# What TensorE waits for in two attention loops: a later exponential in place of a one-element fence

## The chip, the cores and the metric

One Trainium2 chip, all 8 cores, the same program on each with its own batch element of 4096 tokens. The metric is the device time in microseconds of the slowest core, as the median over runs. The span is the time from the first to the last instruction of the profiled execution on the slowest core.

## The reference

For each of 8 batch elements x is 4096 x 1024. First comes full attention with 16 heads of 64, then a two-layer block with windowed attention and a gated feed-forward:

```python
def _L0_attn_ref(query, Wq, Wk, Wv, Wp, bp):
    q = einsum('bnd,hde->bhne', query, Wq) * (1 / sqrt(E))
    k = einsum('bmd,hde->bhme', query, Wk); v = einsum('bmd,hde->bhme', query, Wv)
    attn = softmax(einsum('bhne,bhme->bhnm', q, k), axis=-1)
    out = einsum('bhnm,bhme->bnhe', attn, v)
    return dot(swapaxes(out, -1, -2).reshape(B, N, E * H), Wp) + bp
def _layer(x, ...):                      # DEPTH = 2, 8 heads of 64, window 512
    h = shift_token(x); q, k, v = split(h @ wqkv, 3)
    q, k = rotary_xpos(l2norm(q) * qs, l2norm(k) * ksc)
    x = x + local_attention(q, k, v) @ wo          # own window and the one before it
    a, g = split(layernorm(shift_token(x)) @ w1 + b1, 2)
    return x + (a * gelu(g)) @ w2 + b2
x = x + _L0_attn_ref(_layernorm(x), ...)
x = x + _L0_ffn_ref(_layernorm(x), ...)            # two times _layer
```

## The kernel before, in words

The program is written engine by engine. Each call of `op` (line 131) appends one instruction to the list of one engine, in the order of the code, and an engine works its list in order. Engines meet on counting semaphores: T for TensorE (`'T'`), V for VectorE (`'V'`), S for ScalarE (`'S'`). A `wait` list names a semaphore and the value that it has to reach. `self.val('S')` is the value that S will have after everything put on ScalarE's list so far. On VectorE and ScalarE `op` adds two things to each instruction: it waits until the one before it on the same engine is complete, and it raises the engine's own semaphore by one when it is complete. All instructions have line 150 in the profile, since `op` issues them, so they are told apart by their tiles.

A fence (`sfence` on ScalarE, `vfence` on VectorE) copies one element of the tile `fsc` onto another. A consumer that waits for the value after the fence waits for the instruction ahead of it and for the copy.

Stage A (`_stage_a`, from line 364 on) normalises x into eight tiles h, then goes over 4 groups of 4 heads. Per group it loads the weights, computes K (tiles KTg) and V (tile Vg) for all 4096 tokens, and goes over 8 blocks of 512 queries. Per block it projects Q for two pairs of heads (tile Qg) and runs one attention loop per pair. After both loops come eight output projections (Ost with Wpg), each followed by work of VectorE and a DMA.

An attention loop has 32 chunks of 128 keys, with mc as the counter. Per chunk:

- Q·K: two matmuls (KTg with Qg, 64 rows each, one for each head) into pb1 for even chunks and pb3 for odd ones. They wait for the value `sexp[mc - 2]`, since that exponential read the same buffer.
- Exponential: one ACTIVATE of 128 x 1024 from the buffer into Pa (even) or Pb (odd), which waits for the Q·K pair and for the P·V pair of chunk mc - 2, which read the same tile.
- P·V: two matmuls (Vg with Pa or Pb) that accumulate in pb5 and pb6 over all chunks. They wait for `sexp[j]`.

The code of iteration mc puts Q·K of chunk mc on TensorE's list, then P·V of chunk mc - 1. The list so reads QK0, QK1, PV0, QK2, PV1, QK3, PV2 and so on. `sexp[mc]` is set to the value after a fence (line 601). When the loop is over, VectorE takes the reciprocal of the row of sums (RECIPROCAL into drow), TensorE spreads it over 64 partitions, and VectorE scales the result; so for both heads.

Stage F (`_ffn_layer`, from line 741 on, called once for each of two layers) goes over 8 windows of 512 tokens, with projections, norms and rotation, and then 4 pairs of heads of local attention. Per pair there are 8 chunks of 128 keys, 4 in window 0. Per chunk k: two Q·K matmuls (kf with qf) into pb5 and pb6 for even k, into pb1 for odd k, which wait for `sexp_l[k - 2]`; two additions of a 128 x 128 mask by VectorE in place and a VectorE fence; two ACTIVATEs (into the Ph tiles, 128 to 512 columns each) that wait for this fence; a ScalarE fence, whose value is `sexp_l[k]` (line 1100). After the last chunk TensorE waits for `self.val('S')` (line 1103) and does all P·V matmuls of the pair. Then come reciprocal, spreading and scaling as in stage A. The rest of a layer is the output projection, statistics, and a feed-forward over 16 spans of 256 tokens.

Of the kernel before, what the change touches and what calls it, by code (L numbers as in the profile page):

```python
# [8 lines left out]
F32 = mybir.dt.float32  # L9
# [88 lines left out]
class MK:  # L98
# [106 lines left out]
    def build(self):  # L205
        nc = self.nc
        with self.es:
            self._declare_dram()
            self._globals()
            blk = self.es.enter_context(nc.Block())  # L210
            self._stage_a()
            if self.stage in ('F0', 'F0q'):
                self._ffn_layer(0)
            elif self.stage not in ('A', 'A0'):
                self._ffn_layer(0)
                self._ffn_layer(1)
            self._finish()
            with nc.allow_low_precision(reason="bf16 matmul operands by design"):
                for tag, attr in [('T', 'tensor'), ('V', 'vector'), ('S', 'scalar'),
                                  ('G', 'gpsimd'), ('Y', 'sync')]:  # L220
                    fns = self.q[tag]
                    def body(eng, fns=fns):
                        for fn in fns:
                            fn(eng)
                    getattr(blk, attr)(body)
        return nc
# [137 lines left out]
    def _stage_a(self):  # L364
# [10 lines left out]
        pOa, pOb, pm = self.pb5, self.pb6, self.pb7  # L375
# [5 lines left out]
        stA = self.stA = contextlib.ExitStack()  # L381
# [10 lines left out]
        for s in range(8):  # L392
# [11 lines left out]
            for c in range(NCH):  # L404
                for ms in range(4):
                    st = (s == 0 and c == 0 and ms == 0)
# [8 lines left out]
                            inc=(('T', 1) if last else None))  # L415
# [15 lines left out]
        for s in range(8):  # L431
# [14 lines left out]
            for c in range(NCH):  # L446
# [4 lines left out]
                        inc=(('V', 1) if c == NCH - 1 else None))  # L451
# [14 lines left out]
        Vg4 = Vg.rearrange("p (m h e) -> p m h e", h=4, e=65)  # L466
# [5 lines left out]
        Pa = self.sbuf('Pa', [128, 1024], BF16, st=stA)  # L472
        Pb = self.sbuf('Pb', [128, 1024], BF16, st=stA)
        dn = self.sbuf('dn', [64, 512], F32, st=stA)
        drow = self.sbuf('drow', [1, 512], BF16, st=stA)
        Ost = self.sbuf('Ost', [128, 2 * 512], BF16, st=stA)
        ysb = [self.sbuf(f'ysb{i}', [128, 512], F32, st=stA) for i in range(2)]
        yac = [self.sbuf(f'yac{i}', [128, 512], F32, st=stA) for i in range(2)]
# [12 lines left out]
        for grp in range(ngrp):  # L491
# [71 lines left out]
            for qb in range(NQB):  # L563
                if qb == 1:
                    self.canary(2 + grp * 3)
                for p in range(2):
                    for c in range(NCH):
                        self.op('T', 'matmul', pm[:, :], Wq_g[c][:, p * 128:(p + 1) * 128],
                                h[c][:, qb * 512:(qb + 1) * 512],
                                start=(c == 0), stop=(c == NCH - 1),  # L570
                                inc=(('T', 1) if c == NCH - 1 else None))
# [4 lines left out]
                for p in range(2):  # L576
                    sexp = {}
                    tavm = {}
                    p0exp = self.val('S')
                    for mc in range(33):  # L580
                        if mc < 32:
                            Sp = pb1 if mc % 2 == 0 else pb3
                            Pj = Pa if mc % 2 == 0 else Pb
                            wS = [('S', sexp[mc - 2])] if mc >= 2 else [('S', p0exp)]
                            self.op('T', 'matmul', Sp[:, 0:512],
                                    KT[p][0:64, mc * 128:(mc + 1) * 128],
                                    Qg[0:64, p * 512:(p + 1) * 512],
                                    start=True, stop=True, tile_position=(0, 0),
                                    wait=wS)
                            self.op('T', 'matmul', Sp[:, 512:1024],  # L590
                                    KT[p][64:128, mc * 128:(mc + 1) * 128],
                                    Qg[64:128, p * 512:(p + 1) * 512],
                                    start=True, stop=True, tile_position=(64, 0),
                                    inc=('T', 1))
                            ts = self.val('T')
                            we = [('T', ts)]
                            if mc - 2 in tavm:
                                we.append(('T', tavm[mc - 2]))
                            self.op('S', 'activation', Pj[:, :], Sp[:, :], AF.Exp,
                                    scale=0.125, wait=we)  # L600
                            sexp[mc] = self.sfence()
                        if mc >= 1:
                            j = mc - 1
                            Pj = Pa if j % 2 == 0 else Pb
                            self.wait('T', 'S', sexp[j])
                            self.op('T', 'matmul', pOa[0:65, :],
                                    Vg4[:, j, 2 * p, :], Pj[:, 0:512],
                                    start=(j == 0), stop=(j == 31))
                            self.op('T', 'matmul', pOb[0:65, :],
                                    Vg4[:, j, 2 * p + 1, :], Pj[:, 512:1024],  # L610
                                    start=(j == 0), stop=(j == 31),
                                    inc=('T', 1))
                            tavm[j] = self.val('T')
                    tav = self.val('T')
                    for hh, pO in ((0, pOa), (1, pOb)):
                        self.op('V', 'reciprocal', drow[0:1, :], pO[64:65, :],
                                wait=[('T', tav)] if hh == 0 else None, inc=('V', 1))
                        vr1 = self.vfence()
                        self.op('T', 'matmul', pm[0:64, 0:512], self.ones1b[0:1, 0:64],
                                drow[0:1, :], start=True, stop=True,  # L620
                                wait=[('V', vr1)], inc=('T', 1))
                        tb1 = self.val('T')
                        self.op('V', 'tensor_copy', dn[:, :], pm[0:64, 0:512], wait=[('T', tb1)])
                        self.op('V', 'tensor_tensor',
                                Ost[hh * 64:(hh + 1) * 64, p * 512:(p + 1) * 512],
                                pO[0:64, :], dn[:, :], op=ALU.mult, inc=('V', 1))
                    self.wait('T', 'V', self.vfence())
# [21 lines left out]
                for oc in range(8):  # L649
                    for p in range(2):  # L650
# [3 lines left out]
                                inc=(('T', 1) if p == 1 else None))  # L654
# [17 lines left out]
                    else:  # L672
# [29 lines left out]
                        for ms in range(4):  # L702
                            st = h0_first[0]
# [4 lines left out]
                                    start=st, stop=False, skip_group_check=True)  # L708
                            self.op('T', 'matmul', pb0[:, 96 + qb * 4 + ms:97 + qb * 4 + ms],
                                    x1s[b][:, ms * 128:(ms + 1) * 128], self.onesb[:, :],  # L710
                                    start=False, stop=bend, skip_group_check=True,
                                    inc=(('T', 1) if ms == 3 else None))
                        x1_sums_t[b] = self.val('T')
                        if self.stage == 'X1' and grp == 3 and qb == 0 and oc == 1:
# [6 lines left out]
                                    inc=('V', 1))  # L721
# [8 lines left out]
                                    inc=('V', 1))  # L730
# [10 lines left out]
    def _ffn_layer(self, l):  # L741
# [27 lines left out]
        sb = lambda nm, shp, dt: self.sbuf(f'L{l}{nm}', shp, dt, st=stF)  # L769
# [45 lines left out]
        Ph = [sb(f'Ph{i}', [128, 8 * 512], BF16) for i in range(2)]  # L815
        dnl = sb('dnl', [64, 512], F32)
        drl = sb('drl', [1, 512], BF16)
        Ow = sb('Ow', [128, 4 * 512], BF16)
        za = sb('za', [128, 8 * 513], F32)
        za3 = za.rearrange("p (c n) -> p c n", n=513)  # L820
# [19 lines left out]
        for w in range(self.nwin):  # L840
# [18 lines left out]
            if l == 0:  # L859
# [13 lines left out]
                else:  # L873
                    self.op('T', 'matmul', pb1[:, 0:512], self.ones1b[:, :],
                            self.arow0[0:1, w * 512 - 1:(w + 1) * 512 - 1],
                            start=True, stop=True, wait=tw)
                    self.op('T', 'matmul', pb1[:, 512:513], self.ones1b[:, :],
                            self.arow0[0:1, (w + 1) * 512 - 1:(w + 1) * 512],
                            start=True, stop=True)
                    self.op('T', 'matmul', pb3[:, 0:512], self.ones1b[:, :],  # L880
                            self.brow0[0:1, w * 512 - 1:(w + 1) * 512 - 1],
                            start=True, stop=True)
                    self.op('T', 'matmul', pb3[:, 512:513], self.ones1b[:, :],
                            self.brow0[0:1, (w + 1) * 512 - 1:(w + 1) * 512],
                            start=True, stop=True, inc=('T', 1))
# [6 lines left out]
                            inc=('V', 1))  # L892
                for c in range(NCH):
# [7 lines left out]
                            inc=(('V', 1) if c == NCH - 1 else None))  # L901
            else:
                for c in range(NCH):
# [4 lines left out]
                            inc=(('V', 1) if c == NCH - 1 else None))  # L908
# [9 lines left out]
            for pc in range(4):  # L918
                for part, bid, pbank, dst in ((0, 0, pb1, qraw), (1, 1, pb3, kraw)):
                    if bid in bank_free:  # L920
                        self.wait('T', 'V', bank_free[bid])
                    for c in range(NCH):
# [3 lines left out]
                                start=(c == 0), stop=(c == NCH - 1),  # L926
                                inc=(('T', 1) if c == NCH - 1 else None))
# [8 lines left out]
            for ms in range(4):  # L936
# [4 lines left out]
                for c in range(NCH):  # L941
# [3 lines left out]
                            start=(c == 0), stop=(c == NCH - 1),  # L945
                            inc=(('T', 1) if c == NCH - 1 else None))
# [11 lines left out]
            for pc in range(4):  # L958
# [3 lines left out]
                        inc=(('V', 1) if pc == 3 else None))  # L962
            self.wait('T', 'V', self.vfence())
            for pc in range(4):
                for ms in range(4):
# [5 lines left out]
                            inc=(('T', 1) if pc == 3 and ms == 3 else None))  # L971
# [17 lines left out]
            for pc in range(4):  # L989
# [10 lines left out]
                if b in free_rq:  # L1000
                    wq.append(('V', free_rq[b]))
                self.op('T', 'matmul', qn_t[b], self.bd[:, :], q2b[:, :],
                        start=True, stop=True, wait=wq, inc=('T', 1))
# [7 lines left out]
                        start=True, stop=True, wait=[('S', sqn)], inc=('T', 1))  # L1011
# [33 lines left out]
            for pc in range(4):  # L1045
# [3 lines left out]
                sexp_l = {}  # L1049
                for k, (mc, qlo, qhi) in enumerate(chunks(w)):  # L1050
# [8 lines left out]
                            start=True, stop=True, tile_position=(0, 0), wait=wS)  # L1059
# [3 lines left out]
                            start=True, stop=True, tile_position=(64, 0),  # L1063
# [25 lines left out]
                    if first_exp:  # L1089
# [7 lines left out]
                            SB[:, qlo:qhi], AF.Exp,  # L1097
                            scale=rksrc[:, (pc * 4 + vsrc) * 2 + 1:(pc * 4 + vsrc) * 2 + 2],
                            inc=('S', 1))
                    sexp_l[k] = self.sfence()  # L1100
                if self.sub < 46:
                    continue
                self.wait('T', 'S', self.val('S'))
                for qsub in range(4):
                    mcs = [mc for (mc, qlo, qhi) in chunks(w) if qlo <= qsub * 128 < qhi]
                    for ki, mc in enumerate(mcs):
# [340 lines left out]
```

How the kernel before makes its waits and increments, by code:

```python
        def fn(e):  # L147
            for sm, v in wait:
                e.wait_ge(semh[sm], v)
            instr = getattr(e, meth)(*a, **kw)
            for sm, k in incv:
                instr.then_inc(semh[sm], k)
# [2 lines left out]
    def wait(self, eng, sem, v):  # L155
        semh = self.semh
        self.emit(eng, lambda e: e.wait_ge(semh[sem], v))
# [12 lines left out]
        def fn(e):  # L170
            for sm, v in toks:
                e.wait_ge(semh[sm], v)
```

## Time and profile before

| what | us |
|---|---|
| runs of the kernel before, median of 2 | 12647.35 (12560.37 to 12734.32) |
| profiled execution | 12526.19 |
| its span on the slowest core (core 2) | 12524.6 |
| spans of the 8 cores | 12383.2 to 12524.6 |
| TensorE matmuls, busy | 6169.9 (49%) |
| VectorE, busy | 4236.7 (34%) |
| ScalarE, busy | 3670.8 (29%) |

The granted clock of TensorE is 0.720 in the mean over the slowest core's span (1.00 is 2.4 GHz, 0.50 is 1.2 GHz). In the profile PE is TensorE, PEld its weight loads, DVE is VectorE, ACT is ScalarE. "pb<-Qg,KTg" is a matmul of Q·K in stage A, "pb<-Pa,Vg" and "pb<-Pb,Vg" are P·V, "fsc<-fsc" is a fence. Busy time is the sum of the instructions' durations; the idle time before a group is what its engine waited just ahead of it, with the instruction that ended the wait behind the arrow. The duration of matmuls is modelled at its end.

### The profile page before, as it was taken

The page shows a single profiled execution, that of the slowest core. Times are in us where ns is not written, and L with a number is a line of the kernel's source. Part 1 is how long each engine was busy: PE and PEld are TensorE (multiplying, and loading weights), DVE is VectorE, ACT ScalarE, POOL GpSimd, SP SyncE. Part 2 cuts the span into 40 slices and gives each one's busy share as a digit, 9 for nine tenths or more (in the row PEclk, how much of TensorE's full clock was granted, in tenths as well). Part 3 has the DMA queues.
Part 4 walks back from the last instruction along what each step waited for, and adds up shares of the span by engine and source line. Part 5 has one row for each costly group of instructions (what it writes and reads, how often), then busy time and mean ns, then how long its engine had stood idle before and what let it go on. Part 6 is the DMA issues. An engine that isn't in the chain of part 4 may idle for free.

```text
span 12524.6 us, 129835 instructions; the slowest of 8 cores (12383.2 to 12524.6 us)
## 1 busy us (share of the span) xinstructions
PE 6169.9 (49%) x36558; PEld 3126.1 (25%) x36694; DVE 4236.7 (34%) x8932; ACT 3670.8 (29%) x7204; POOL 270.0 (2%) x406
## 2 busy tenths in 40 slices
PE   3555555555554554433333334777633333346776
PEld 1111211111111211111111113666511111135665
DVE  5121211122111222235555552333244444423333
ACT  0555355534444344421111120111112112201111
POOL 0000000000000000000000000000000000000000
PEclk9887787778777777765555556888855555567888
DMA  3000010110111011110010003000010000041110
GB/s 115 14 14 14 21 14 14 14 21 12 16 17 17 25 41 41 41 41 17 17 34 17 17 17 75 28 22 28 25 38 17 23 28 17 17 86 40 35 38 28
DMA packets 237216, 361.47 MB, mean 29 GB/s; under 512 B 27664, under 2 KB 122512, under 8 KB 234468
## 3 DMA queue, kind: packets, MB, share of 16 engines
q0 software_dynamic: 51968, 101.01, 4.9%
q1 hardware_dynamic: 120036, 168.23, 4.4%
q10 hardware_dynamic: 64512, 83.91, 1.9%
q8 instruction: 315, 5.16, 0.2%
q14 instruction: 385, 3.15, 0.1%
HBM read 269.23 MB, written 134.35 MB: 32 GB/s over the span
## 4 chain that ended last, share of the span: by engine, by line
PE 33%; DVE 24%; ACT 23%; issue 10%; DMA 8%; DVEq 1%; ACTq 1%; SPq 0%; POOL 0%; POOLq 0%
PE pb L150 33%; ACT Pa L150 8%; ACT Pb L150 8%; ACT fsc L150 4%; DVE drow L150 3%; DVE fsc L150 2%; DVE L1drl L150 2%; DVE L0drl L150 2%; DMA yacc<-ysb 2%; ACT L0Ph L150 1%; ACT L1Ph L150 1%; DVE L0tmp L150 1%; DVEq L149 1%; DVE pb L150 1%; DVE ysb L150 1%
## 5 line engine op out<-in xcount | busy, mean ns | idle before, releaser
L150 ACT ACTIVATE Pa<-pb 128x1024 bf16<-128x1024 f32 x1024 | 1049.3, 1025 | 2566.2 <-PE pb L150 2481.0
L150 DVE RECIPROCAL drow<-pb 1x512 bf16<-1x512 f32 x128 | 429.0, 3352 | 3034.2 <-PE pb L150 3027.6
L150 ACT ACTIVATE Pb<-pb 128x1024 bf16<-128x1024 f32 x1024 | 1049.3, 1025 | 116.0 <-PE pb L150 22.8
L150 PE MATMUL pb<-Pa,Vg 128*65 128x512 bf16 x2048 | 655.9, 403 | 514.1 <-ACT fsc L150 507.8
L150 PE MATMUL pb<-Qg,KTg 64*128 64x512 bf16 x4096 | 843.7, 414 | 113.2 <-DVE fsc L150 113.2
L150 PE MATMUL pb<-Pb,Vg 128*65 128x512 bf16 x2048 | 653.6, 402 | 468.0 <-ACT fsc L150 466.1
L150 PE MATMUL pb<-L0dh,L0dw 128*128 128x256 bf16 x5632 | 725.4, 286 | 170.9 <-DVE fsc L150 170.9
L150 PE MATMUL pb<-L1dh,L1dw 128*128 128x256 bf16 x5632 | 722.5, 286 | 170.9 <-DVE fsc L150 170.9
L150 ACT COPY fsc<-fsc 1x1 f32<-1x1 f32 x3320 | 631.3, 190 | 291.3 <-ACT L0dgelb L150 1.1
L150 PEld LDWEIGHTS pb<-L0dh,L0dw 128*128 128x128 bf16 x5632 | 576.1, 103 | 271.8 <-issue 181.5
L150 PEld LDWEIGHTS pb<-L1dh,L1dw 128*128 128x128 bf16 x5632 | 574.7, 102 | 270.7 <-issue 181.5
L150 DVE COPY fsc<-fsc 1x1 f32<-1x1 f32 x3161 | 448.5, 142 | 335.0 <-DVE pb L150 2.5
L150 PEld LDWEIGHTS pb<-Qg,KTg 64*128 64x128 bf16 x4096 | 202.5, 94 | 1019.0 <-issue 1018.6
L150 PE MATMUL pb<-Ost,Wpg 128*128 128x512 bf16 x472 | 243.8, 611 | 370.3 <-DVE fsc L150 368.3
L150 DVE TENSOR_TENSOR pb<-pb,M_sb 128x128 f32<-128x128 f32 x960 | 287.7, 300 | 407.1 <-PE pb L150 347.8
L150 ACT ACTIVATE L0Ph<-pb,L0rk 128x512 bf16<-128x512 f32 (+1 forms) x480 | 253.2, 527 | 568.6 <-DVE fsc L150 537.1
L150 ACT ACTIVATE L1Ph<-pb,L1rk 128x512 bf16<-128x512 f32 (+1 forms) x480 | 253.2, 527 | 567.0 <-DVE fsc L150 516.0
L150 PE MATMUL pb<-L0du,L0dw 128*128 128x256 bf16 (+1 forms) x2816 | 376.4, 278 | 18.2 <-DVE fsc L150 18.2
L150 PE MATMUL pb<-L1du,L1dw 128*128 128x256 bf16 (+1 forms) x2816 | 374.7, 277 | 17.4 <-DVE fsc L150 17.2
L150 PE MATMUL pb<-drow,ones1b 1*64 1x512 bf16 x128 | 76.9, 601 | 603.1 <-DVE fsc L150 603.1
L150 PEld LDWEIGHTS pb<-Pa,Vg 128*65 128x65 bf16 x2048 | 149.2, 112 | 823.7 <-issue 823.7
L150 PEld LDWEIGHTS pb<-Pb,Vg 128*65 128x65 bf16 x2048 | 148.4, 111 | 773.1 <-issue 773.1
(263 smaller groups left out, 7215.9 us busy)
## 6 DMA issues: line engine op xcount, KB each, us to landing
yacc<-ysb POOLq DMA_DIRECT2D x192, 256.0 KB, 4.1
xspan<-xT SPq DMA_DIRECT2D x16, 2048.0 KB, 9.9
yac<-yacc SPq DMA_DIRECT2D x64, 256.0 KB, 3.6
xsp<-xT SPq DMA_DIRECT2D x64, 256.0 KB, 4.0
R<-x1f ACTq DMA_DIRECT2D x64, 256.0 KB, 3.9
RA<-L0za ACTq DMA_DIRECT2D x64, 256.0 KB, 2.7
RZ<-L0dzot ACTq DMA_DIRECT2D x128, 128.0 KB, 1.7
RA<-L1za ACTq DMA_DIRECT2D x64, 256.0 KB, 3.0
```

What stands on the lines that cost most here:

```text
L149: e.wait_ge(semh[sm], v)
L150: instr = getattr(e, meth)(*a, **kw)
```

## The change

In the attention loop of stage A `sexp[mc]` is the value right after the exponential, with no fence; one fence remains, after the last chunk, as `sexp[32]`. The P·V matmuls are written ahead of Q·K in the code of an iteration, for chunk mc - 2 in place of mc - 1, and wait for `sexp[j + 1]`, the exponential of the next chunk. The loop has one more turn. In local attention `sexp_l[k]` is likewise the value right after the second ACTIVATE, and one fence is put behind the last chunk. Two tiles of one row, `drowf` and `drlf`, are allocated and not used. The test that selects the full program is written as `self.stage == 'full'`, which holds here.

```diff
@@ _stage_a
+        drowf = self.sbuf('drowf', [1, 512], F32, st=stA)
...
-                    for mc in range(33):
+                    for mc in range(34):
+                        if mc >= 2:
+                            j = mc - 2
+                            Pj = Pa if j % 2 == 0 else Pb
+                            self.wait('T', 'S', sexp[j + 1] if j + 1 in sexp else sexp[j])
+                            self.op('T', 'matmul', pOa[0:65, :],
+                                    Vg4[:, j, 2 * p, :], Pj[:, 0:512],
+                                    start=(j == 0), stop=(j == 31))
+                            self.op('T', 'matmul', pOb[0:65, :],
+                                    Vg4[:, j, 2 * p + 1, :], Pj[:, 512:1024],
+                                    start=(j == 0), stop=(j == 31),
+                                    inc=('T', 1))
+                            tavm[j] = self.val('T')
                         if mc < 32:
...
                             self.op('S', 'activation', Pj[:, :], Sp[:, :], AF.Exp,
                                     scale=0.125, wait=we)
-                            sexp[mc] = self.sfence()
-                        if mc >= 1:
-                            j = mc - 1
-                            Pj = Pa if j % 2 == 0 else Pb
-                            self.wait('T', 'S', sexp[j])
...
+                            sexp[mc] = self.val('S')
+                            if mc == 31:
+                                sexp[32] = self.sfence()
@@ _ffn_layer
+        drlf = sb('drlf', [1, 512], F32)
...
-                    sexp_l[k] = self.sfence()
+                    sexp_l[k] = self.val('S')
...
-                self.wait('T', 'S', self.val('S'))
+                self.wait('T', 'S', self.sfence())
```

TensorE's list, at the start of a loop of stage A. It is the same before and after:

```order
L150 MATMUL pb<-Qg,KTg 128x512 [waits S]
L150 MATMUL pb<-Qg,KTg 128x512
L150 MATMUL pb<-Pa,Vg 65x512 [waits S]
L150 MATMUL pb<-Pa,Vg 65x512
L150 MATMUL pb<-Qg,KTg 128x512 [waits S]
L150 MATMUL pb<-Qg,KTg 128x512
L150 MATMUL pb<-Pb,Vg 65x512 [waits S]
L150 MATMUL pb<-Pb,Vg 65x512
```

No matmul moved. The first pair here is Q·K of chunk 1, then P·V of chunk 0, Q·K of chunk 2, P·V of chunk 1. What differs is the value of S that each P·V pair waits for: before, that after the exponential of its own chunk and its fence; after, that of the exponential of the following chunk.

ScalarE's list at the start of the first loop, before:

```order
L150 ACTIVATE Pa<-pb 128x1024 [waits T,S]
L150 COPY fsc<-fsc 1x1 [waits S]
L150 ACTIVATE Pb<-pb 128x1024 [waits T,S]
L150 COPY fsc<-fsc 1x1 [waits S]
L150 ACTIVATE Pa<-pb 128x1024 [waits T,S]
```

And after, around the end of a loop (the copy is the one fence that is left, and the next loop begins behind it):

```order
L150 ACTIVATE Pb<-pb 128x1024 [waits T,S]
L150 ACTIVATE Pa<-pb 128x1024 [waits T,S]
L150 ACTIVATE Pb<-pb 128x1024 [waits T,S]
L150 COPY fsc<-fsc 1x1 [waits S]
L150 ACTIVATE Pa<-pb 128x1024 [waits T,S]
```

31 of the 32 fences of each loop are gone. ScalarE's list for a head pair of the local attention in window 0, after:

```order
L150 ACTIVATE L0Ph<-pb,L0rk 128x512 x2
L150 ACTIVATE L0Ph<-pb,L0rk 128x384 x2
L150 ACTIVATE L0Ph<-pb,L0rk 128x256 x2
L150 ACTIVATE L0Ph<-pb,L0rk 128x128 x2
L150 COPY fsc<-fsc 1x1
```

Before, such a copy stood behind each of the four rows of ACTIVATEs. On ScalarE 2400 rows are gone in all; on the other engines none is added or removed.

## Rows read from the trace of the kernel before

**Rows 1.** Costliest groups: out<-in shapes xcount | busy us, mean ns | idle before, releaser
```profile
L150 ACT ACTIVATE Pa<-pb 128x1024 bf16<-128x1024 f32 x1024 | 1049.3, 1025 | 2566.2 <-PE pb L150 2481.0
...
L150 ACT ACTIVATE Pb<-pb 128x1024 bf16<-128x1024 f32 x1024 | 1049.3, 1025 | 116.0 <-PE pb L150 22.8
...
L150 PE MATMUL pb<-Qg,KTg 64*128 64x512 bf16 x4096 | 843.7, 414 | 113.2 <-DVE fsc L150 113.2
...
L150 ACT COPY fsc<-fsc 1x1 f32<-1x1 f32 x3320 | 631.3, 190 | 291.3 <-ACT L0dgelb L150 1.1
```

**Rows 2.** Timeline, a loop of stage A: start us, us, engine, operation [idle before <-releaser]
```profile
3011.86 1.02 ACT L150 ACTIVATE Pa<-pb 128x1024 bf16<-128x1024 f32 x1
...
3011.91 0.59 PE L150 MATMUL pb<-Pb,Vg 128*65 128x512 bf16 x2 [0.30 <-ACT fsc L150]
...
3012.44 0.39 PE L150 MATMUL pb<-Qg,KTg 64*128 64x512 bf16 x2
3012.97 0.19 ACT L150 COPY fsc<-fsc 1x1 f32<-1x1 f32 x1
3013.26 1.02 ACT L150 ACTIVATE Pb<-pb 128x1024 bf16<-128x1024 f32 x1
...
3013.31 0.59 PE L150 MATMUL pb<-Pa,Vg 128*65 128x512 bf16 x2 [0.48 <-ACT fsc L150]
```

**Rows 3.** A stretch inside that loop: window, busy (count) of each engine, PEclk, DMA
```profile
3011.30:3048.90 37.60, 24.66 (x110) 6.33 (x108) 0.00 (x0) 32.59 (x55) 0.00 (x0) 1.00 0.00 1
```

**Rows 4.** Timeline, where two loops begin and end
```profile
3005.30 0.61 PE L150 MATMUL pb<-Qg,KTg 64*128 64x512 bf16 x4 [1.36 <-DVE fsc L150]
3005.84 1.02 ACT L150 ACTIVATE Pa<-pb 128x1024 bf16<-128x1024 f32 x1 [48.36 <-PE pb L150]
...
3051.89 3.35 DVE L150 RECIPROCAL drow<-pb 1x512 bf16<-1x512 f32 x1 [46.84 <-PE pb L150]
...
3064.47 1.03 PE L150 MATMUL pb<-Qg,KTg 64*128 64x512 bf16 x4 [2.14 <-DVE fsc L150]
3065.23 1.02 ACT L150 ACTIVATE Pa<-pb 128x1024 bf16<-128x1024 f32 x1 [14.25 <-PE pb L150]
...
3111.80 3.35 DVE L150 RECIPROCAL drow<-pb 1x512 bf16<-1x512 f32 x1 [47.59 <-PE pb L150]
```

**Rows 5.** Timeline, first steps of the second loop
```profile
3066.34 0.19 ACT L150 COPY fsc<-fsc 1x1 f32<-1x1 f32 x1
...
3066.67 1.03 PE L150 MATMUL pb<-Pa,Vg 128*65 128x512 bf16 x2 [1.17 <-ACT fsc L150]
...
3067.64 0.61 PE L150 MATMUL pb<-Qg,KTg 64*128 64x512 bf16 x2
...
3068.46 1.02 ACT L150 ACTIVATE Pa<-pb 128x1024 bf16<-128x1024 f32 x1 [0.54 <-PE pb L150]
```

**Rows 6.** Stretches, columns as in rows 3: that loop, output projections, local attention
```profile
3069.90:3072.75 2.85, 2.85 (x8) 0.56 (x8) 0.00 (x0) 2.24 (x3) 0.00 (x0) 0.50 0.02 6
3120.00:3150.00 30.00, 11.77 (x24) 2.23 (x25) 9.56 (x21) 0.00 (x0) 6.90 (x8) 0.50 0.50 68
6912.00:6925.00 13.00, 2.97 (x13) 0.90 (x14) 5.12 (x21) 9.96 (x24) 0.00 (x0) 0.50 0.00 1
```

**Rows 7.** Timeline, one head pair of the local attention, layer 0
```profile
6912.03 0.83 ACT L150 ACTIVATE L0Ph<-pb,L0rk 128x128 bf16<-128x128 f32 x2 [18.98 <-DVE fsc L150]
...
6913.28 0.50 PE L150 MATMUL pb<-L0qf,L0kf 64*128 64x384 bf16 x2 [2.26 <-ACT fsc L150]
...
6914.69 0.61 PE L150 MATMUL pb<-L0qf,L0kf 64*128 64x512 bf16 x2 [0.91 <-ACT fsc L150]
...
6915.06 1.25 ACT L150 ACTIVATE L0Ph<-pb,L0rk 128x384 bf16<-128x384 f32 x2 [0.51 <-DVE fsc L150]
...
6918.62 1.47 ACT L150 ACTIVATE L0Ph<-pb,L0rk 128x512 bf16<-128x512 f32 x2 [0.19 <-DVE fsc L150]
...
6923.69 0.83 ACT L150 ACTIVATE L0Ph<-pb,L0rk 128x128 bf16<-128x128 f32 x2 [0.20 <-DVE fsc L150]
```

More of the change, by code:

```diff
@@ L213, in build @@
                 self._ffn_layer(0)
-            elif self.stage not in ('A', 'A0'):
+            elif self.stage == 'full':
                 self._ffn_layer(0)
@@ L600, in _stage_a @@
                                     scale=0.125, wait=we)
-                            sexp[mc] = self.sfence()
-                        if mc >= 1:
-                            j = mc - 1
-                            Pj = Pa if j % 2 == 0 else Pb
-                            self.wait('T', 'S', sexp[j])
[L606 to L613, printed above, removed]
+                            sexp[mc] = self.val('S')
+                            if mc == 31:
+                                sexp[32] = self.sfence()
                     tav = self.val('T')
```

## The prediction

> **What bounds the kernel now.** I read, in this order, the page's busy shares and costliest groups, the timeline of one attention loop, the busy time and granted clock of chosen stretches, then the ends of loops and one piece of the local attention. [rows 1] are totals: the 2048 wide exponentials of stage A take 1049.3 us in Pa and 1049.3 us in Pb, the tiny ScalarE copies ("fences", tile fsc) 631.3 us in 3320 pieces. Pb waits 116.0 us in all; the 2566.2 us before Pa are nearly all the pauses between loops. So within a loop ScalarE hardly waits. The timeline shows it step by step [rows 2]: exponential at 3011.86, fence at 3012.97, next exponential at 3013.26: 1.40 us a step, made of 1.02 us exponential, 0.09, 0.19 fence, 0.09. TensorE does its two P·V and two Q·K matmuls for an earlier chunk beside that and then sits: it is behind a fence each time ("0.48 <-ACT fsc"). In a long stretch of such steps the clock is fully granted, with TensorE busy 24.66 of 37.60 us and ScalarE 32.59 [rows 3]. A loop runs from its first exponential to the reciprocal that ends it: 3005.84 to 3051.89, 46.05 us, and 3065.23 to 3111.80, 46.57 us [rows 4]; mean 46.31. There are 4 groups x 8 query blocks x 2 pairs = 64 of them, 2964 us of the span of 12524.6.
>
> **Stage A, the wait.** TensorE's order of matmuls is the same before and after; what is new is the value waited for. Before, P·V of chunk j waited for exponential j and its fence, while exponential j+1 ran beside it. Now P·V(j) waits for exponential j+1. TensorE works in order, and Q·K(j+2) stands behind P·V(j) on it, and exponential j+2 needs Q·K(j+2). So each step is one chain with nothing beside it: exponential j+1, P·V(j), Q·K(j+2), exponential j+2. The fence of 0.28 us (with its gap) goes, but its cost is small beside the overlap that goes.
>
> The price of a chained step depends on the clock. At half clock [rows 5] shows it: fence ends 3066.34+0.19 = 3066.53, P·V starts 3066.67 (0.14 later), Q·K 3067.64 (0.97 later), and the exponential that waited for it ("0.54 <-PE pb") 3068.46, 0.82 later. With 1.02 for the exponential itself: 1.02 + 0.14 + 0.97 + 0.82 = 2.95 us. At full clock P·V to Q·K is 3012.44 - 3011.91 = 0.53 [rows 2], Q·K to exponential 3005.84 - 3005.30 = 0.54 at a loop's start [rows 4], so 1.02 + 0.14 + 0.53 + 0.54 = 2.23 us.
>
> Which clock? At the full one TensorE would stream the same four matmuls per step, but in 2.23 us instead of 1.40, so it is idle for most of the step. Stretches where TensorE works in such short bursts between waits are at half clock: the output projections, 11.77 us busy of 30.00, and local attention, 2.97 of 13.00, both at a granted 0.50 [rows 6]. Once low, the chained step keeps it about as idle: in each 2.95 us it has 1.6 us of work by [rows 5]. The return to full clock in the loops of before came only after a stretch in which TensorE worked nearly without a pause (2.85 busy of 2.85 us [rows 6]), which the chain no longer offers. I take 1.2 GHz throughout the loops, 2.95 us.
>
> A loop then is: first two exponentials back to back, 1.02 + 0.09 = 1.11; 30 chained steps, 88.5; the last exponential, 1.02; then both P·V pairs of chunks 30 and 31 are still to do, 0.14 + 0.97 + 1.03 and 0.18 to the reciprocal, 2.32. Sum 92.95, against 46.31: +46.64, times 64 = **+2985 us**. The wait of the last P·V for the one remaining fence (0.28 after the exponential) is hidden by the P·V before it.
>
> Bounds: the delay from the end of a wide exponential to TensorE is not in the trace. The nearest are 0.09 (exponential to fence) and 0.21 (a Q·K pair's modelled end, 3067.64 + 0.61 = 3068.25, to the exponential, 3068.46); I take the 0.14 of fence to P·V, the same pair of engines. Q·K to exponential may be 0.76, as at a loop's start (3064.47 to 3065.23 [rows 4]), instead of 0.82. Over 64 x 30 steps that is -211 us at the low end, +134 at the high.
>
> The Trainium skill bears on the choice of clock. "TensorE: Matmul & The Clock Gate", section "Why this matters for your kernels", has it that what sends the clock back is long idle gaps between bursts of matmuls, longer than any inside a chained step here. By that rule the loops would stay at 2.4 GHz. The trace speaks against it: the clock is half in local attention, where gaps before matmuls are 0.91 to 2.26 us [rows 7].
>
> **Local attention.** 7 of 8 fences go for each head pair of a window (3 of 4 in window 0): per layer 4 x (3 + 7 x 7) = 208, both layers 416; with 31 x 64 = 1984 in stage A that makes 2400, leaving 920 copies. One pair's exponentials run from 6912.03 to 6923.69 + 0.83 = 6924.52, 12.49 us [rows 7]. Two limits alternate: ScalarE's own sequence, and the chain exponential k, Q·K(k+2), two mask additions, VectorE's fence, exponential k+2, 6912.86 to 6915.06 = 2.20 us for the third, 6916.31 to 6918.62 = 2.31 us for the fifth. The removed fence is 0.28 of each (0.42 from exponential to matmul, 6912.86 to 6913.28; 0.14 without it). Walking the eight chunks with 1.92 to 2.03 us for the chain of the middle ones, somewhat less for the last two (narrower matmuls), and 0.09 between exponentials, they start at 0, 0.92, 2.75, 4.09, 6.03, 7.59, 9.31 and 10.54, and the last ends at 11.4 instead of 12.49: 1.1 us. 7 x 4 x 2 = 56 such pairs, and 8 short ones at half: **-66 us**. It is on the path, since the P·V matmuls wait for the last fence and all engines for them. Bounds: 0, if the mask chain hides all, and 416 x 0.28 = -116.
>
> The two new one-row tiles are never used, and the changed stage test is the same for the full program: 0, at both ends.
>
> **Sum.** 12526.2 (the profiled execution; span 12524.6) + 2985 - 66 = 15,445. The runs shown have a median of 12647.35, 121 above the profiled one, the lower of them 34 above. I take 15,445 + 34, about 15,480.
>
> **Rivals.**
> 1. *The clock stays at 2.4 GHz in the chained loop.* For it: TensorE is granted 1.00 with pauses of 0.48 us per step already [rows 2, 3]. Against it: the pauses grow to over half the step, and other bursty stretches are at 0.50 [rows 6]. Loop: 1.11 + 30 x 2.23 + 1.02 + 0.14 + 0.53 + 0.59 + 0.18 = 70.5, +24.2 x 64 = +1546; time 14,040.
> 2. *The clock alternates inside loops.* If each level holds half of it: about 14,760.
> 3. *Not slower.* The fence was the only cost and the P·V wait isn't on ScalarE's path: if TensorE had Q·K(j+2) out before exponential j+1 ended, ScalarE would step in 1.02 + 0.09 = 1.11 us. Place: the 64 loops; price 31 x (1.11 - 1.40) x 64 = -575, with local attention's -66: 11,920. It decides from the point at which a second Q·K chunk stands ahead of the P·V wait on TensorE. Against: the order has exactly one chunk ahead, and [rows 2] show TensorE waiting for ScalarE, not the reverse. The Trainium skill points this way: "Perfetto Trace Analysis", section "Identifying the Most-Contended Engine", says to work on the engine with the highest occupancy. In the loop that is ScalarE, and the trace agrees (32.59 of 37.60 us); by it the removed copies alone would count.
>
> **Numbers.** The forecast's mechanism (chain, half clock) 0.88; rival 1 0.04; rival 2 0.05; rival 3 0.03. The forecast's own range: 15,445 - 211 - 50 = 15,184 to 15,445 + 134 + 66 + 121 = 15,766; trimmed at its thin ends to 15,200 to 15,750, which holds about 0.8 of everything. A measurement of this kernel tells about 2% from no change; slower by over 2%: 0.96, within 2%: 0.01, faster by over 2%: 0.03.
>
> **What would show it.** In the profile after: exponentials 2.95 us apart, ScalarE's idle time before both Pa and Pb near 1.9 us a step, TensorE's P·V waiting for Pa or Pb itself instead of fsc; TensorE's clock in tenths 5 in stage A's slices; Q·K and P·V matmuls longer in the mean than Q·K's 414 ns; fsc copies on ScalarE x920; a pair's exponentials in local attention spanning 11.4 us. Wrong if steps are 2.2 us (clock), 1.1 us (no chain), or if stage F changes by more than 120 us.

## The result and the profile after

The changed kernel takes 15481.04 us (median of 11 runs, 15391.18 to 15605.09), the kernel before 12557.58 us (median of 10 runs, 12528.31 to 12734.32). The ratio is 1.2333, with a 95% interval of 1.2291 to 1.2374: slower by nearly a quarter. In some executions the cores of one die show a lower granted clock and take some per cent longer; the medians in this document count every run, the ratios leave those executions out. The profiled execution took 15563.55 us, with a span of 15562.0 us on core 7.

The page of the changed kernel, the clock row of the 40 slices and the groups that answer to [rows 1]. Columns as there:

```profile
PEclk8555555555555555555555555556788555557777
...
L150 DVE RECIPROCAL drow<-pb 1x512 bf16<-1x512 f32 x128 | 429.0, 3352 | 6022.0 <-PE pb L150 6015.4
L150 ACT ACTIVATE Pa<-pb 128x1024 bf16<-128x1024 f32 x1024 | 1048.2, 1024 | 4372.2 <-PE pb L150 4372.2
L150 PE MATMUL pb<-Pa,Vg 128*65 128x512 bf16 x2048 | 1058.0, 619 | 1456.7 <-ACT Pb L150 1456.7
L150 PE MATMUL pb<-Pb,Vg 128*65 128x512 bf16 x2048 | 1060.6, 620 | 1330.0 <-ACT Pa L150 1330.0
L150 ACT ACTIVATE Pb<-pb 128x1024 bf16<-128x1024 f32 x1024 | 1048.2, 1024 | 1859.0 <-PE pb L150 1853.1
L150 PE MATMUL pb<-Qg,KTg 64*128 64x512 bf16 x4096 | 1224.8, 599 | 113.3 <-DVE fsc L150 113.3
```

Three things are to be read here. The exponentials themselves cost what they did (1024 ns each), but the idle time before Pb, which has no pauses between loops in it, went from 116.0 to 1859.0 us. The P·V matmul that reads Pa now waits for the exponential of Pb, and the other way round: the releaser is the next chunk's exponential, where it was a fence. And the Q·K matmul went from 414 to 599 ns, with the clock at 5 tenths in every slice of stage A but the first. (A slice is 389 us here, and the last loop ends at about 8430 us, in the 22nd.)

The timeline of one loop, its beginning and its end, answers to [rows 2, 4, 5]:

```profile
3035.07 1.02 ACT L150 ACTIVATE Pa<-pb 128x1024 bf16<-128x1024 f32 x1 [47.71 <-PE pb L150]
...
3041.27 0.61 PE L150 MATMUL pb<-Qg,KTg 64*128 64x512 bf16 x2
3042.09 1.02 ACT L150 ACTIVATE Pb<-pb 128x1024 bf16<-128x1024 f32 x1 [1.93 <-PE pb L150]
3043.26 1.03 PE L150 MATMUL pb<-Pa,Vg 128*65 128x512 bf16 x2 [1.38 <-ACT Pb L150]
3044.23 0.61 PE L150 MATMUL pb<-Qg,KTg 64*128 64x512 bf16 x2
3045.05 1.02 ACT L150 ACTIVATE Pa<-pb 128x1024 bf16<-128x1024 f32 x1 [1.93 <-PE pb L150]
...
3125.07 1.02 ACT L150 ACTIVATE Pb<-pb 128x1024 bf16<-128x1024 f32 x1 [1.93 <-PE pb L150]
...
3126.23 1.03 PE L150 MATMUL pb<-Pa,Vg 128*65 128x512 bf16 x2 [1.38 <-ACT Pb L150]
3127.06 1.06 PE L150 MATMUL pb<-Pb,Vg 128*65 128x512 bf16 x2
3128.30 3.35 DVE L150 RECIPROCAL drow<-pb 1x512 bf16<-1x512 f32 x1 [94.24 <-PE pb L150]
```

Only one of the two engines works at a time. ScalarE ends at 3042.09 + 1.02 = 3043.11, P·V starts at 3043.26, Q·K at 3044.23, the next exponential at 3045.05: 2.96 us from one exponential to the next, 1.93 of it idle on ScalarE. The loop takes 3128.30 - 3035.07 = 93.23 us; the mean over the 64 loops of this core is 93.06, against 46.39 on the slowest core of before. 64 x 46.67 = 2987 us.

A stretch inside this loop, with the columns of [rows 3]: TensorE is busy half the time, and the granted clock is 0.50, where it was 1.00.

```profile
3040.00:3120.00 80.00, 42.55 (x108) 7.92 (x108) 0.00 (x0) 27.62 (x28) 0.00 (x0) 0.50 0.00 0
```

In local attention, here on core 2 of the changed kernel, the pair runs from 9609.18 to 9619.79 + 0.83 = 9620.62, 11.44 us, against 12.49 in [rows 7]. All 56 full pairs have a mean of 11.48 us, against 12.61 before:

```profile
9609.18 0.83 ACT L150 ACTIVATE L0Ph<-pb,L0rk 128x128 bf16<-128x128 f32 x2 [18.28 <-DVE fsc L150]
...
9610.15 0.51 PE L150 MATMUL pb<-L0qf,L0kf 64*128 64x384 bf16 x2 [1.97 <-ACT L0Ph L150]
...
9611.93 2.81 ACT L150 ACTIVATE L0Ph<-pb,L0rk 128x384 bf16<-128x384 f32 x4 [0.71 <-DVE fsc L150]
...
9615.21 2.81 ACT L150 ACTIVATE L0Ph<-pb,L0rk 128x512 bf16<-128x512 f32 x4 [0.47 <-DVE fsc L150]
...
9619.79 0.83 ACT L150 ACTIVATE L0Ph<-pb,L0rk 128x128 bf16<-128x128 f32 x2 [0.26 <-DVE fsc L150]
```

The matmul follows the exponential after 9610.15 - 9610.01 = 0.14 us, as taken, and what ScalarE waits for between chunks is VectorE's fence, as in [rows 7]: the chain exponential, Q·K, mask still sets part of the pace, without ScalarE's fence in it.

### The profile page after: what moved, and what is told of

Its sections match the earlier page's. It is cut to its first block, busy times and chain, and to the rows that moved or that the text cites. A ratio compares the mean times of both kernels' runs of the same rounds, so it can differ in the third digit from the quotient of the medians.

```text
span 15562.0 us, 125171 instructions; the slowest of 8 cores (15425.3 to 15562.0 us)
## 1 busy us (share of the span) xinstructions
PE 7527.8 (48%) x36694; PEld 3313.3 (21%) x36694; DVE 4236.6 (27%) x8932; ACT 3211.1 (21%) x4804; POOL 270.0 (2%) x406
## 4 chain that ended last, share of the span: by engine, by line
PE 46%; DVE 20%; ACT 16%; issue 9%; DMA 7%; DVEq 1%; ACTq 1%; SPq 0%; POOL 0%; POOLq 0%
PE pb L150 46%; ACT Pb L150 7%; ACT Pa L150 7%; DVE drow L150 3%; DVE fsc L150 2%; DVE L0drl L150 1%; DVE L1drl L150 1%; DMA yacc<-ysb 1%; DVE L0tmp L150 1%; ACT L0Ph L150 1%; DVE pb L150 1%; ACT L1Ph L150 1%; DVEq L149 1%; ACTq L149 1%; DVE ysb L150 1%
## 5 line engine op out<-in xcount | busy, mean ns | idle before, releaser
L150 ACT ACTIVATE Pa<-pb 128x1024 bf16<-128x1024 f32 x1024 | 1048.2, 1024 | 4372.2 <-PE pb L150 4372.2
L150 PE MATMUL pb<-Pa,Vg 128*65 128x512 bf16 x2048 | 1058.0, 619 | 1456.7 <-ACT Pb L150 1456.7
L150 PE MATMUL pb<-Pb,Vg 128*65 128x512 bf16 x2048 | 1060.6, 620 | 1330.0 <-ACT Pa L150 1330.0
L150 ACT ACTIVATE Pb<-pb 128x1024 bf16<-128x1024 f32 x1024 | 1048.2, 1024 | 1859.0 <-PE pb L150 1853.1
L150 PE MATMUL pb<-Qg,KTg 64*128 64x512 bf16 x4096 | 1224.8, 599 | 113.3 <-DVE fsc L150 113.3
L150 PE MATMUL pb<-L1dh,L1dw 128*128 128x256 bf16 x5632 | 799.6, 306 | 170.9 <-DVE fsc L150 170.9
L150 PE MATMUL pb<-L0dh,L0dw 128*128 128x256 bf16 x5632 | 742.8, 291 | 170.9 <-DVE fsc L150 170.9
L150 PEld LDWEIGHTS pb<-L1dh,L1dw 128*128 128x128 bf16 x5632 | 611.9, 109 | 307.9 <-issue 181.5
L150 PEld LDWEIGHTS pb<-L0dh,L0dw 128*128 128x128 bf16 x5632 | 584.6, 104 | 280.2 <-issue 181.4
L150 PEld LDWEIGHTS pb<-Pa,Vg 128*65 128x65 bf16 x2048 | 192.8, 144 | 1953.3 <-issue 1953.3
L150 PEld LDWEIGHTS pb<-Pb,Vg 128*65 128x65 bf16 x2048 | 203.1, 146 | 1819.6 <-issue 1819.6
L150 PE MATMUL pb<-L1du,L1dw 128*128 128x256 bf16 (+1 forms) x2816 | 415.8, 298 | 16.4 <-DVE fsc L150 16.3
L150 PE MATMUL pb<-L0du,L0dw 128*128 128x256 bf16 (+1 forms) x2816 | 384.4, 282 | 17.4 <-DVE fsc L150 17.4
L150 PEld LDWEIGHTS pb<-L1du,L1dw 128*128 128x128 bf16 (+1 forms) x2816 | 295.5, 106 | 81.5 <-issue 25.3
```

Of the source, the lines that this page charges most:

```text
L150: instr = getattr(e, meth)(*a, **kw)
```

## The experiments

The theory: P·V of chunk j waits for exponential j+1, Q·K(j+2) stands behind it on TensorE, and exponential j+2 needs that, so the step is a chain; the chain leaves TensorE idle enough for the clock to stay at half, which makes it longer still. Removing fences by itself is a gain. The rivals: the fences gone do harm by themselves; the P tiles bind rather than the order on TensorE; the clock is a symptom and not a cost.

All loops below are means over 64 loops of one core, from the first exponential to the reciprocal. Each ratio is against the kernel before on the same chip, whose median was 12590.34 us beside the first four kernels, 12512.36 beside the next four and 12598.99 beside the last. The step is the median over a loop's steps; where two lengths take turns, 1.12 and 1.18 us, it is their mean.

| kernel | us, median | loop, us | step, us | clock in loops | head pair, us |
|---|---|---|---|---|---|
| before | 12557.58 | 46.4 | 1.39 | 0.93 | 12.61 |
| changed | 15481.04 | 93.1 | 2.95 | 0.50 | 11.48 |
| stage A's part alone | 15494.42 | 93.1 | 2.95 | 0.50 | 12.61 |
| local attention's part alone | 12520.69 | 46.4 | 1.39 | 0.92 | 11.48 |
| own exponential waited for | 12094.27 | 38.7 | 1.15 | 0.94 | 11.48 |
| fences back in the chain | 15450.23 | 93.3 | 2.95 | 0.50 | 11.48 |
| filler matmuls | 14228.6 | 73.2 | 2.29 | 0.98 | 11.48 |
| Q·K ahead, two P tiles | 14277.28 | 75.1 | 2.35 | 0.51 | 11.48 |
| four P tiles, order kept | 15386.28 | 92.9 | 2.95 | 0.50 | 11.48 |
| Q·K ahead, four P tiles | 12028.35 | 39.4 | 1.15 | 0.92 | 11.48 |
| the same, own exponential | 11918.15 | 37.2 | 1.12 | 0.93 | 11.48 |

**The two parts alone.** First stage A's part, with local attention put back:

```diff
-                    sexp_l[k] = self.val('S')
+                    sexp_l[k] = self.sfence()
...
-                self.wait('T', 'S', self.sfence())
+                self.wait('T', 'S', self.val('S'))
```

Expected: 

> Stage A's part of the change alone; local attention keeps its fences. Theory (chain in stage A costs about 2985 us, local attention's fences are worth 66 to 85 us): 15,550 us, ratio to the kernel before 1.239, loops of stage A 92.9 us from first exponential to reciprocal, a head pair of local attention 12.6 us. Rival (the stage F part costs something too, or the loops share the loss with it): below 15,400.

Measured: ratio 1.2405 (1.2316 to 1.2494), loops of 93.1 us, head pairs of 12.61 us. The loss is stage A's. The medians do not resolve the 66 us: this one is 13 above the changed kernel's and not 70, in a spread of 177 us.

Then the local attention part alone, the reverse edit on the kernel before:

```diff
-                    sexp_l[k] = self.sfence()
+                    sexp_l[k] = self.val('S')
...
-                self.wait('T', 'S', self.val('S'))
+                self.wait('T', 'S', self.sfence())
```

Expected: 

> The local attention part alone; stage A as before. Theory: faster by 1.1 us on each of 56 full head pairs and 0.6 on 8 short ones, 66 us, up to 85: ratio 0.993 to 0.995, about 12,480 us; pairs 11.5 us instead of 12.6. Rival (the time is given back by what follows on VectorE): pairs shorter, ratio 1.000.

Measured: ratio 0.9961 (0.9905 to 1.0016). The time is inconclusive, since the interval takes in 1.000 as well as the 0.995 that was expected. The trace does show the pairs at 11.48 us instead of 12.61, 56 x 1.13 and 8 x 0.59 = 68 us. The spans of the cores show that this gain reaches the end of the program: where a core's granted clock was 0.728 or more in its span, the median is 12,349 us here (35 spans) and 12,417 in the kernel before on the same chip (57 spans), 69 us more.

**The wait and the fence apart.** The changed kernel with one index different:

```diff
-                            self.wait('T', 'S', sexp[j + 1] if j + 1 in sexp else sexp[j])
+                            self.wait('T', 'S', sexp[j])
```

Expected: 

> The changed kernel, but each P.V pair waits for the value right after its own exponential (j) instead of the next one's (j+1); no fences. Theory (the wait for j+1 is the whole loss; removing fences alone is a gain): the chain exponential, P.V, Q.K, exponential then spans two steps, 2.23 us at full clock, so a step is 1.11 to 1.13 us, a loop 37 us, time 11,880 us, ratio 0.946, clock 1.00 in the loops. Rival (the fences gone are what slows it, by some cost of a wait on a wide exponential): above 15,000. Second rival (clock low in loops): 1.48 us a step, about 12,600.

Measured: 12094.27 us, 0.961 of the median of before on that chip (12590.34). With the runs chosen as for the other ratios it is 0.967 (means of 12084.5 and 12499.5; there is no interval). The whole loss went and a gain stands in its place, so removed fences do no harm. The size was missed by some 200 us. One part is the step, 1.15 and not 1.12 us. The timeline, here of core 7, shows why, and how two steps overlap:

```profile
2700.72 1.02 ACT L150 ACTIVATE Pb<-pb 128x1024 bf16<-128x1024 f32 x1 [0.15 <-ACT Pa L150]
...
2701.23 0.39 PE L150 MATMUL pb<-Qg,KTg 64*128 64x512 bf16 x2
2701.84 1.02 ACT L150 ACTIVATE Pa<-pb 128x1024 bf16<-128x1024 f32 x1
...
2701.88 0.59 PE L150 MATMUL pb<-Pb,Vg 128*65 128x512 bf16 x2 [0.26 <-ACT Pb L150]
...
2702.41 0.39 PE L150 MATMUL pb<-Qg,KTg 64*128 64x512 bf16 x2
...
2703.01 1.02 ACT L150 ACTIVATE Pb<-pb 128x1024 bf16<-128x1024 f32 x1 [0.15 <-ACT Pa L150]
```

P·V of the one chunk runs beside the exponential of the other. From Q·K to its exponential are 0.60 to 0.61 us, where the sum had used the 0.54 of a loop's start. Two steps are 1.02 + 0.14 + 0.53 + 0.60 = 2.29 us, and the rows have 2703.01 - 2700.72 = 2.29. That is above twice ScalarE's own 1.11, so the chain and not ScalarE sets the pace in every other step. The larger part is the start of the loop: the second to fifth steps take 1.68, 1.53, 1.32 and 1.21 us in the mean of the 64 loops, 1.3 us above 4 x 1.12, and the granted clock in them is 0.59, 0.53, 0.75 and 0.92. The longer loop (38.7 against 37) is 64 x 1.7 = 109 us of the miss. The rest lies behind the last loop, in what the slowest core, core 0, does in 7123 us at a mean granted clock of 0.651 and core 7 in 6919 us at 0.674. The spans of cores 4 to 7 are 11,861 to 11,895 us.

**Fences in the chain.** The changed kernel with a fence behind each exponential, and the waited value left as it is:

```diff
                             sexp[mc] = self.val('S')
-                            if mc == 31:
-                                sexp[32] = self.sfence()
+                            sexp[32] = self.sfence()
```

Expected: 

> The changed kernel with a fence put back behind each exponential of stage A, while P.V still waits for the value right after exponential j+1. Theory (in the chain ScalarE is idle for 1.9 us a step, so a fence of 0.28 us there costs nothing): 15,480 us, within 0.5% of the changed kernel. Rival (fences are on the path in any order): + 0.28 x 30 x 64 = 540, 16,020.

Measured: 15450.23 us, ratio 1.2338 (1.2226 to 1.2449), beside the 1.2333 of the changed kernel. ScalarE's row for the exponential shows where the fences went, as idle time before Pb that got smaller, 1597.6 us instead of 1859.0, at the same step:

```profile
L150 ACT ACTIVATE Pb<-pb 128x1024 bf16<-128x1024 f32 x1024 | 1047.6, 1023 | 1597.6 <-PE pb L150 1591.7
```

The difference, 261.4 us over 960 waits, is 0.27 us each, a fence with its gap. In the chain a fence is free: what was removed had no price there. Outside it, one is not: the first two exponentials of a loop, which wait for no P·V, are 1.40 us apart here and 1.12 in the changed kernel, and the loop is 0.28 us longer.

**The clock.** Three matmuls of 128 x 512 behind each Q·K pair, into a PSUM tile that the loop does not use. They add nothing to the result:

```diff
                             ts = self.val('T')
+                            for _f in range(3):
+                                self.op('T', 'matmul', pm[:, :], KT[p][:, 0:128],
+                                        h[0][:, 0:512], start=True, stop=True)
```

Expected: 

> The changed kernel with three extra matmuls of 128x512 behind each Q.K pair of stage A, into a PSUM tile that the loop does not use; they add no result. They keep TensorE busy while it would wait for the exponential. Theory (0.72 us of each chained step is the half clock): the granted clock in the loops rises to 1.00 or near it, the step is 2.23 us, time about 14,060 us although TensorE does more work. Rival (the step is long for another reason, such as semaphore delays, and the clock is only a symptom): 2.95 us or more a step, 15,500 or above.

Measured: 14228.6 us, 1250 us less than the changed kernel with more work on TensorE; the loops alone give 64 x 19.9 = 1270. The stretch and the timeline inside a loop:

```profile
3020.00:3080.00 60.00, 43.36 (x182) 11.64 (x182) 0.00 (x0) 26.71 (x27) 0.00 (x0) 1.00 0.00 1
```

```profile
3029.48 0.59 PE L150 MATMUL pb<-Pa,Vg 128*65 128x512 bf16 x2 [0.63 <-ACT Pb L150]
3030.01 0.39 PE L150 MATMUL pb<-Qg,KTg 64*128 64x512 bf16 x2
3030.33 0.82 PE L150 MATMUL pb<-h,KTg 128*128 128x512 bf16 x3
3030.61 1.02 ACT L150 ACTIVATE Pa<-pb 128x1024 bf16<-128x1024 f32 x1 [1.27 <-PE pb L150]
3031.78 0.59 PE L150 MATMUL pb<-Pb,Vg 128*65 128x512 bf16 x2 [0.63 <-ACT Pa L150]
```

The fillers run while the exponential does and are done before the next P·V. With the clock at 1.00, 2.4 GHz, the step is 3031.78 - 3029.48 = 2.30 us. So 0.65 us of the 2.95 is the half clock, and the chain at full clock still costs 2.30 against the 1.39 of before. The rival in which the clock is a symptom falls.

**Order and tiles apart.** There are two ties between P·V(mc-2) and exponential mc: Q·K(mc) stands behind it on TensorE, and the exponential overwrites the P tile that it reads. In the changed kernel with Q·K put ahead, the first tie is cut alone; `ts + 1` is the value of T after P·V(mc-2):

```diff
-                        if mc >= 2:
-                            j = mc - 2
-                            Pj = Pa if j % 2 == 0 else Pb
-                            self.wait('T', 'S', sexp[j + 1] if j + 1 in sexp else sexp[j])
...
                         if mc < 32:
...
-                            if mc - 2 in tavm:
-                                we.append(('T', tavm[mc - 2]))
+                            if mc >= 2:
+                                we.append(('T', ts + 1))
...
+                        if mc >= 2:
+                            j = mc - 2
+                            Pj = Pa if j % 2 == 0 else Pb
+                            self.wait('T', 'S', sexp[j + 1] if j + 1 in sexp else sexp[j])
...
```

The whole block with the two P·V matmuls moved; it is the same text behind the exponential as it was ahead of Q·K.

Expected: 

> The changed kernel with Q.K of chunk mc put ahead of P.V of chunk mc-2 on TensorE, still waiting for exponential mc-1, and two P tiles as before, so that exponential mc waits for P.V(mc-2). Theory: Q.K leaves the chain, P.V stays in it by the P tile: at half clock 1.02 + 0.14 + 1.03 + 0.21 = 2.40 us a step, time 14,420; at full clock 1.96, 13,570. Rival (order on TensorE alone makes the chain): 1.12 us a step, 11,880.

Measured: 14277.28 us, ratio 1.1415 (1.1270 to 1.1560), and a step of 2.35 us in the timeline:

```profile
3080.34 1.02 ACT L150 ACTIVATE Pa<-pb 128x1024 bf16<-128x1024 f32 x1 [1.33 <-PE pb L150]
3081.51 1.03 PE L150 MATMUL pb<-Pb,Vg 128*65 128x512 bf16 x2 [0.78 <-ACT Pa L150]
3082.47 0.61 PE L150 MATMUL pb<-Qg,KTg 64*128 64x512 bf16 x2
3082.69 1.02 ACT L150 ACTIVATE Pb<-pb 128x1024 bf16<-128x1024 f32 x1 [1.33 <-PE pb L150]
```

The exponential starts 0.22 us after Q·K of the next chunk has begun, so it is no longer that matmul that it waits for but the P·V pair before it, 1.18 us after its start. Only P·V is left in the chain, at the half clock.

The second tie alone, four P tiles and the order kept:

```diff
-                            Pj = Pa if mc % 2 == 0 else Pb
+                            Pj = Pq[mc % 4]
...
-                            if mc - 2 in tavm:
-                                we.append(('T', tavm[mc - 2]))
+                            if mc - 4 in tavm:
+                                we.append(('T', tavm[mc - 4]))
```

Expected: 

> The changed kernel with four P tiles in place of two, order on TensorE unchanged (P.V ahead of Q.K). Theory: exponential j+2 still waits for Q.K(j+2), which stands behind P.V(j) on TensorE, so nothing changes: 2.95 us a step, 15,480. Rival (the P tiles are what binds): below 14,500.

Measured: 15386.28 us (one run), step 2.95 us. More tiles alone do nothing; the order on TensorE is a full chain by itself.

Both ties cut, by the two edits together, while P·V still waits for exponential j+1:

Expected: 

> Q.K ahead of P.V and four P tiles, P.V still waits for exponential j+1. Theory: both ties are cut though the late wait stays, the remaining chain spans two steps (1.02 + 0.14 + 0.53 + 0.54 = 2.23), 1.11 to 1.13 us a step at full clock, about 11,880 us, ratio 0.946. Rival (waiting for j+1 costs by itself): above 12,600.

Measured: 12028.35 us, ratio 0.9605 (0.9508 to 0.9702), steps of 1.12 and 1.18 us in turn. Waiting for the later exponential has a small price of its own, which the next kernel shows; it is what stands behind the wait that has the large one. As in the kernel that waits for its own exponential, the 0.61 us from Q·K to exponential makes the step longer than the 1.12 expected.

**The best order.** The last kernel, with P·V waiting for its own exponential:

Expected: 

> Q.K ahead of P.V, four P tiles, and P.V waits for its own exponential, with local attention's fences removed. Theory: the chain over two steps is now exponential, Q.K, exponential (1.02 + 0.15 + 0.61 = 1.78), below ScalarE's own 2 x 1.11, so ScalarE sets the pace: 1.11 us a step, a loop near 36.5 us against 38.7 and 39.4 of the two fastest so far, 64 x 2.2 = 140 us less, about 11,900 us, ratio 0.948. Rival (ScalarE's own sequence costs more than 1.11 or the clock dips bind): 1.17 us a step, no gain over the kernel with the own exponential waited for.

Measured: 11918.15 us, ratio 0.9465 (0.9411 to 0.9518), the fastest here, faster than both kernels. Its loop is 2.2 us shorter than that of the kernel just above (37.2 against 39.4), from which it differs in the waited value alone: 64 x 2.2 = 140 us is what the later wait costs when order and tiles leave room for it. Inside a loop:

```profile
3043.90 1.02 ACT L150 ACTIVATE Pd<-pb 128x1024 bf16<-128x1024 f32 x1
3043.95 0.39 PE L150 MATMUL pb<-Qg,KTg 64*128 64x512 bf16 x2 [0.17 <-ACT Pc L150]
3044.27 0.62 PE L150 MATMUL pb<-Pc,Vg 128*65 128x512 bf16 x2
3045.01 1.02 ACT L150 ACTIVATE Pa<-pb 128x1024 bf16<-128x1024 f32 x1
```

ScalarE steps in 1.11 us with no wait on TensorE; Q·K starts 0.05 us after the exponential and P·V follows. The loop is 37.2 us and not 36.5. Two stretches of this kernel, the start of the loop and the part shown, tell why:

```profile
3018.00:3028.00 10.00, 6.78 (x20) 1.40 (x20) 1.54 (x4) 5.12 (x5) 0.00 (x0) 0.50 0.00 0
3040.00:3050.00 10.00, 8.44 (x37) 2.38 (x36) 0.00 (x0) 9.17 (x10) 0.00 (x0) 1.00 0.00 0
```

The first steps run at half clock, where the matmuls of a step take longer than the exponential, until the clock comes up.

## Why the prediction was right

- *The chain.* Forecast: exponential, P·V, Q·K, exponential with nothing beside it, since TensorE's order puts Q·K(j+2) behind the wait. The timeline shows it, the releasers name it, and the pair of kernels that cut the two ties one by one shows that the order alone suffices.
- *The price of a step.* Forecast 2.95 us from four pieces of [rows 5]; measured 2.95. The one piece not in the trace of before, from the end of a wide exponential to P·V, was taken as 0.14 and is 0.15 (3043.11 to 3043.26).
- *The clock.* Forecast 1.2 GHz throughout the loops; measured 0.50. The filler experiment gives the price: 2.95 against 2.30 us. On core 7, 25 of the 64 loops began at the full clock, and it fell in all of them within 3.6 us of the first exponential; the longest gap before a matmul ahead of such a fall is 2.22 us, and those in the chain are 1.38. The kernel before has the same fall: on core 2, 30 loops began at the full clock, all lost it within 3.2 us, and 62 of the 64 had it 20 us into the loop. So the chain does not bring the clock down, it keeps it from coming back, as the forecast had it; in the changed kernel it came back in none of the 64. The rule of the Trainium skill that was weighed ("TensorE: Matmul & The Clock Gate", section "Why this matters for your kernels"), which ties the fall to longer gaps than these, does not agree with the trace. The prediction set it aside on a row that does not test it: ahead of the pair in [rows 7] TensorE waits 5.49 us at a time, up to its matmul at 6907.66.
- *The loop.* Forecast 92.95 us and +2985 in all; measured 93.06 and +2987. The tail came out 0.1 us shorter than taken (2.22 instead of 2.32 after the last exponential), the first step and the others up to 0.01 longer.
- *Local attention.* Forecast -66 us, pairs of 11.4 us; measured pairs of 11.48, 68 us by their sum, and 69 us by the core spans of the kernel with this part alone. The 920 copies left are counted in the trace.
- *The sum.* Forecast 15,480, measured 15,481. The two terms, 2985 - 66 = 2919 us, meet a difference of the medians of 2923. The closeness to 1 us is luck: the runs spread over 214 us, and the profiled execution, 15,563, is 118 above the sum of 15,445 that was made for it. What it has more is mostly behind the local attention of layer 1, in the feed-forward, which the change does not touch: 1701 us at a mean granted clock of 0.73, against 1560 us at 0.81 in the kernel with the fences back in the chain, which had nearly the same loops and a span of 15382.2 us.
- *Rival 1* had a real price, about 1250 us below the result, and a false condition. The size given for it was 60 ns a step too low, by the 0.54 us from Q·K to exponential, which is 0.61 inside a loop.
- *Rival 3* described what the removal of fences does when the wait is left where it was: 12,094 us where it gave 11,920.

## What to carry to other kernels

A wait costs what is queued behind it on its engine. Before a semaphore value is moved to a later event, list the instructions behind the waiting one and ask which of them that later event's engine needs next; here one chunk of Q·K was queued ahead, and a wait later by one chunk used it up. Slack has to be made in both places, the order of issue and the number of buffers, for either alone left a chain (2.35 and 2.95 us a step). And where the clock follows the engine's activity, as TensorE's does here, such a chain is dearer still: price the step at the clock that its own idle time will bring, and not at that of the kernel before.

## What the runs showed of the hardware that was not expected

- Adding work made the kernel faster: three unused matmuls a step took the granted clock from 0.50 to 1.00 and the time from 15,481 to 14,229 us.
- Each copy of one element on ScalarE, 190 ns and 0.28 us with its gaps, could be dropped in each of 2400 places; in stage A, with the wait left at its own exponential, that is worth 7.7 us in each loop of 46.4, and nothing in the chain of the changed kernel.
- From the start of a Q·K pair to the start of the exponential that waits for it the trace has 0.54 us at a loop's start and 0.61 us behind a P·V pair, both at full clock. What makes the difference was not tried.
